# Attention operand stacks that outlive the projection block: constant rows and the first four units set up while the projection runs

## The reference

```python
x = x + attn0(layernorm(x))   # second norm with ln_g, ln_b inside; 16 heads of 16; causal softmax
x = x + mlp0(layernorm(x))    # 256 -> 2048 -> 256, 4-bit weights with scales, tanh-gelu
x = x + attn1(layernorm(x))   # 4 heads of 64, full softmax
x = x + moe1(layernorm(x))    # 64 experts of width 176, top 6, and a shared expert

# both attentions
Q, K, V = Xn @ Wq + bq, Xn @ Wk + bk, Xn @ Wv + bv
A = softmax(Q @ K.T * scale)              # per head
x = x + (A @ V) @ Wo + bo
```

## Time and profile before

| | us |
|---|---|
| median of 3 runs | 1477.82 |
| profiled execution, its own time | 1485.07 |
| its span, first to last instruction | 1483.2 |
| layer 0: projection block starts, attention block starts | 9.8, 88.7 |
| layer 1: projection block starts, attention block starts | 642, 706.0 |
| PE busy, share of the span | 86% |
| DVE, ACT, POOL | 54%, 29%, 34% |
| mean granted TensorE clock | 0.937 |

### The profile page before, as it was taken

The page is one execution under the profiler, slowest core; times in us unless marked ns, Lnnn a source line. Parts: engine busy times, 40 slices in busy tenths (PEclk is TensorE's granted clock), DMA queues, the critical chain, the costliest instruction groups (busy, mean ns, idle before and its releaser), DMA issues. The chain is left out here.

```text
span 1483.2 us, 22490 instructions
## 1 busy us (share of the span) xinstructions
PE 1268.3 (86%) x6348; PEld 888.1 (60%) x6348; DVE 806.5 (54%) x2185; ACT 431.8 (29%) x847; POOL 502.1 (34%) x602
## 2 busy tenths in 40 slices
PE   3859998987899999978799979748999999999950
PEld 2435555655688888845455565446777676676740
DVE  6747877743544343355445437984545444454437
ACT  1204544554533333222234422101222222222210
POOL 0042332333300000000400000867777777677720
PEclk9968989999999999989799989879999999999985
DMA  5598854800000000025543101019999999999949
GB/s 176 215 210 130 122 82 73 115 9 29 29 1 1 1 0 1 1 96 210 153 113 104 46 32 61 3 47 295 298 300 292 286 285 283 275 286 279 252 142 339
DMA packets 129927, 210.35 MB, mean 142 GB/s; under 512 B 26807, under 2 KB 59563, under 8 KB 129848
## 3 DMA queue, kind: packets, MB, share of 16 engines
q1 hardware_dynamic: 101911, 162.02, 40.8%
q0 software_dynamic: 15264, 34.78, 8.0%
q10 hardware_dynamic: 12672, 12.58, 2.4%
HBM read 168.92 MB, written 48.30 MB: 146 GB/s over the span
## 5 line engine op out<-in xcount | busy, mean ns | idle before, releaser
L1786 PE MATMUL experts_ps_gu<-experts_wgu,experts_xt 128*128 128x352 f32 x636 | 223.0, 473 | 13.7 <-DMA experts_wgu<-L_ffn_w_gate_up 6.3
L912 DVE TENSOR_REDUCE att_mx<-att_ps 128x1 f32<-128x512 f32 (+3 forms) x240 | 151.6, 652 | 87.1 <-PE att_ps L713 52.8
L713 PE MATMUL att_ps<-att_ks,att_qs 96*128 96x512 f32 (+4 forms) x384 | 157.2, 477 | 40.2 <-DMA att_ks<-k_parts 27.4
L1913 POOL DMA_INDIRECT y_parts<-experts_y,moe_target x159 | 161.5, 1015 | 69.2 <-DVE experts_picked L1877 34.9
L1907 POOL DMA_INDIRECT experts_x<-x_rows,moe_source x159 | 157.1, 988 | 62.8 <-issue 51.8
L1829 ACT ACTIVATE experts_xt<-experts_ps_x 128x256 f32<-128x256 f32 x159 | 60.9, 383 | 362.1 <-PE experts_ps_x L1775 362.1
L1807 PE MATMUL experts_ps_y<-experts_wd,experts_ht 96*128 96x256 f32 x636 | 163.4, 379 | 0.0
L1786 PEld LDWEIGHTS experts_ps_gu<-experts_wgu,experts_xt 128*128 128x128 f32 x636 | 111.7, 190 | 85.7 <-ACT experts_xt L1829 33.2
L849 ACT ACTIVATE att_pt<-att_ps 128x1024 f32<-128x1024 f32 (+3 forms) x160 | 121.7, 763 | 135.8 <-PE att_ps L735 135.4
L1860 DVE COPY experts_ht<-experts_ps_h 96x256 f32<-96x256 f32 x159 | 66.9, 421 | 149.5 <-PE experts_ps_h L1796 149.5
L713 PEld LDWEIGHTS att_ps<-att_ks,att_qs 96*128 96x128 f32 (+1 forms) x384 | 80.3, 214 | 92.7 <-issue 55.1
(11 more groups left out here) (217 smaller groups left out, 2265.6 us busy)
## 6 DMA issues: line engine op xcount, KB each, us to landing
experts_wgu<-L_ffn_w_gate_up SPq DMA_DIRECT2D x159, 352.0 KB, 8.7
experts_wd<-L_ffn_w_down SPq DMA_DIRECT2D x159, 176.0 KB
att_qs<-q_parts SPq DMA_DIRECT2D x112, 128.0 KB, 3.4
att_ks<-k_parts SPq DMA_DIRECT2D x112, 128.0 KB, 5.3
combine_got<-y_parts ACTq DMA_DIRECT2D x24, 512.0 KB, 8.8
q_parts<-qkv_hi SPq DMA_DIRECT2D x8, 512.0 KB, 2.9
q_parts<-qkv_lo SPq DMA_DIRECT2D x8, 512.0 KB, 3.7
k_parts<-qkv_hi SPq DMA_DIRECT2D x8, 512.0 KB, 3.4
```

Source lines behind the costliest of these rows:

```text
L713: ins = pe.matmul(out, qs[a][z][0:rows_a, h, i * P:(i + 1) * P], ks[a][z][0:rows_a, h, 0:width(i)], start=a == 0, stop=a == last_part and ...
L912: dve.tensor_reduce(mx[:, hs[0]:hs[-1] + 1, i], ps_1[:, (u.n * ng + g) % 2, 0:len(hs) * width(i)] .rearrange("p (h w) -> p h w", h=len(hs) ...
L1786: ins = pe.matmul(ps_gu[:, u.bank, 0:2 * FE], xt[:, u.bank, k, :], wgu[u.slot][:, k, :], start=k == 0, stop=k == KD - 1)
L1913: pool.indirect_dma_start(out=parts_dram[:, :], out_offset=bass.IndirectOffsetOnAxis(ap=target[:, n:n + 1], axis=0), in_=y[n % L][:, :], i ...
```

## The change

The stacks, `vs`, `w`, `bias` and their semaphores move into a class `Stacks`, allocated before the projection block and freed after the attention block. What was at the start of the attention block is now in the projection block:

```diff
 def project_qkv(..., heads, pitch, stacks, codes=None):
         @block.sync
             sp.dma_start(bv[:, :], w["bv"].partition_broadcast(P)).then_inc(v_weights_loaded, 16)
+            stacks.load_weights(sp)            # bias, w of the output projection
             if codes:
                 codes.load(sp)
...
-            chunks(sp, body)
+            for c in range(NCH):
+                body(c, True)
+                for n in FIRST_UNITS[c]:       # ((), (0, 1), (2, 3), ())
+                    stacks.load(sp, Unit(n))
+                    stacks.load_v(sp, Unit(n))
             sp.wait_ge(qk_stored, 16 * 4 * NCH)
             sp.wait_ge(v_stored, 16 * NCH)
         @block.gpsimd
             for i in range(CT):
                 pool.memset(v4[:, i, :, hd:hd + 1], 1.0).then_inc(v_columns_set, 1)
+            pool.wait_ge(v_columns_set, 1 + CT)
+            stacks.set_rows(pool)
+class Stacks:
+    def set_rows(self, pool):
+        for z in range(SLOTS):
+            for stacks in (self.qs, self.ks):
+                pool.memset(stacks[self.last_part][z][64:P, :, :].bitcast(F32), 0.0).then_inc(self.zero_rows_set, 1)
+        pool.wait_ge(self.zero_rows_set, 2 * SLOTS)
+        for z in range(SLOTS):
+            pool.memset(self.ks[self.last_part][z][NEG_ROW:NEG_ROW + 2, :, :].bitcast(F32), 1.0)\
+                .then_inc(self.rows_set, 1)
+        pool.wait_ge(self.rows_set, SLOTS)
 def attention(...):
         @block.sync
             def body(u):
                 v = u.plus(2)
-                if v.exists():
-                    if u.plus(-2).exists():
-                        sp.wait_ge(s2_done, (u.n - 1) * nx)
-                    load(v)
-                    if u.plus(-2).exists():
-                        sp.wait_ge(pv_done, (u.n - 1) * CT)
-                    load_v(v)
-                if u.n == 0:
-                    sp.dma_start(bias ...); sp.dma_start(w ...)
+                if v.exists() and v.n >= SLOTS:
+                    sp.wait_ge(s2_done, (u.n - 1) * nx)
+                    stacks.load(sp, v)
+                    sp.wait_ge(pv_done, (u.n - 1) * CT)
+                    stacks.load_v(sp, v)
                 load_maxima(u)
...
-            load(Unit(0))
-            load_v(Unit(0))
             loop(body)
         @block.gpsimd
-            set_rows(pool, qs, 0, 0)
-            for z in range(1, SLOTS):
-                set_rows(pool, qs, 0, z)
-                set_rows(pool, ks, 1, z)
         @block.tensor                          # scores_q no longer waits for stack_set
         @block.vector
-            set_rows(dve, ks, 1, 0)
             loop(body)
```

More of the change, by code:

```diff
@@ L467, in low, with __init__, load_weights, load @@
                           self.high_parts[n][:, :, :].bitcast(F32), ALU.subtract).then_inc(self.low_done, 1)
+FIRST_UNITS = ((), (0, 1), (2, 3), ())
+class Stacks:
+    def __init__(self, s, heads, pitch, parts, q_dram, k_dram, v_dram, wo, bo):
+        self.hu, self.hd = heads * UF // D, D // heads
+        self.rows = self.hu * pitch
+        self.parts, self.last_part = parts, len(parts) - 1
+        self.q_dram, self.k_dram, self.v_dram, self.wo, self.bo = q_dram, k_dram, v_dram, wo, bo
+        self.n_loads = sum(len(q) + len(k) for q, k in parts)
+        self.qs, self.ks = ([[s.sbuf(f"{n}s{a}_{z}", [P, self.hu, S], F32R) for z in range(SLOTS)]
+                             for a in range(len(parts))] for n in "qk")
+        self.vs = [s.sbuf(f"vs{z}", [P, CT, self.rows]) for z in range(SLOTS)]
+        self.w = s.sbuf("w", [P, KD, D])
+        self.bias = s.sbuf("bias", [P, D])
+        self.zero_rows_set = s.sem("zero_rows_set")
+        self.rows_set = s.sem("rows_set")
+        self.qk_loaded = [s.sem(f"qk_loaded{z}") for z in range(SLOTS)]
+        self.v_loaded = [s.sem(f"v_loaded{z}") for z in range(SLOTS)]
+        self.w_loaded = s.sem("w_loaded")
+    def set_rows(self, pool):
[7 more added lines that the diff above has]
+        pool.wait_ge(self.rows_set, SLOTS)
+    def load_weights(self, eng):
+        eng.dma_start(self.bias[:, :], self.bo.partition_broadcast(P)).then_inc(self.w_loaded, 16)
+        eng.dma_start(self.w[:, :, :], self.wo.rearrange("(k p) n -> p k n", p=P)).then_inc(self.w_loaded, 16)
+    def load(self, eng, u):
+        z, b, g = u.slot, u.batch, u.g
+        for a, pair in enumerate(self.parts):
+            for dram, stack, blocks in ((self.q_dram, self.qs, pair[0]), (self.k_dram, self.ks, pair[1])):
+                for row, half in blocks:
+                    src = dram[half][g * UF:(g + 1) * UF, b * S:(b + 1) * S]
+                    eng.dma_start(stack[a][z][row:row + self.hd, :, :].bitcast(F32),
+                                  src.rearrange("(h d) t -> d h t", d=self.hd)).then_inc(self.qk_loaded[z], 16)
+    def load_v(self, eng, u):
+        z, b, g = u.slot, u.batch, u.g
+        src = self.v_dram[b * S:(b + 1) * S, g * self.rows:(g + 1) * self.rows]
+        eng.dma_start(self.vs[z][:, :, :], src.rearrange("(j p) f -> p j f", p=P)).then_inc(self.v_loaded[z], 16)
@@ L482, in exists, with attention @@
         return 0 <= self.n < UNITS
[L485 to L493, removed]
+def attention(nc, tag, x_sb, ident, ident_bf, mask_q, stacks, pitch, causal, scale, normed,
+              codes=None, decoder=None, n_decoded=0):
+    hu, hd, rows = stacks.hu, stacks.hd, stacks.rows
+    parts, last_part, n_loads = stacks.parts, stacks.last_part, stacks.n_loads
+    qs, ks, vs, w, bias = stacks.qs, stacks.ks, stacks.vs, stacks.w, stacks.bias
+    qk_loaded, v_loaded = stacks.qk_loaded, stacks.v_loaded
     nt = CT * hu
     nx = nt // 2
-    rows = hu * pitch
-    last_part = len(parts) - 1
-    n_loads = sum(len(q) + len(k) for q, k in parts)
     with ExitStack() as ctx:
@@ L594, in _ @@
         def _(sp):
[L595 to L609, removed]
             def load_maxima(u):
@@ L698, in scores_q @@
                 z = u.slot
-                if step == 0 and part == 0 and not u.plus(-SLOTS).exists():
-                    for sem in stack_set[z]:
-                        pe.wait_ge(sem, 1)
                 if step == 0 and part == 0:
```

47 lines of the change are left out of this document (14 added, 33 removed).

## The result

The changed kernel takes 1499.42 us, the median of 4 runs (1493.48 to 1505.85), beside 1477.71 for the kernel before in the same session: a ratio of 1.0156, 95% interval [1.012, 1.0191]. It is slower, by some 22 us, and lies 0.8 us from the 1498.6 predicted. The terms of the sum did not come out that well: the memsets were put too small, the transfers of layer 0 and layer 1 too large, and the errors cancelled. That the total came so near is luck.

A forecast was written before the change was run, and what follows sets the result against it. PE bounds the kernel, busy 86% of the span, waiting for loads where attention begins. Terms 16.5 - 1.7 + 4.4 + 1.4 + 0.2 = 20.8 us on 1477.82 gave 1498.6, range 1487 to 1518.

The forecast's parts named there:

- Transfers of layer 0: Projection of layer 0: early unit loads delay later stores in one DMA line; first attention matmul at 115.4 against 98.92, +16.5.
- the second pair of units: Layer 0: loads of units 2 and 3, ahead of chunk 3's stores, take 17.6 us of the DMA line.
- The first pair: Layer 0: loads of units 0 and 1, behind chunk 1's stores, take 17.6 us of the DMA line.
- First maxima: Attention of layer 0: the first maxima no longer queue behind unit 3, so PE's 1.67 us wait goes, -1.7.
- Memsets: Early projection: POOL's memsets hold three 4-element DVE operations in layer 0, +1.4; shorter memsets in layer 1, +0.2.
- The halving for the doubt: Layer 0 memset term: half a memset for each of three held operations, halved again to give +1.4.
- Layer 1, +4.4: Attention of layer 1: transfers give -0.95 at the first matmul, but POOL's additions hold DVE, first maxima +4.4 instead.
- POOL's additions: Layer 1: sixteen additions start with the attention block and hold DVE's 4-element operation until the series ends at 722.6.
- If POOL lets DVE in after one addition, layer 1 gives -1: Alternative for layer 1's attention: DVE is not held to the end of POOL's additions, -1 instead of +4.4.
- The rival with memsets to the end of their series: Projections: memsets hold DVE until their series ends, 16.3 + 4.1 in place of 1.6, time 1517.4; chance 0.32.
- The loads slipping in: Both projections: loads run beside stores without delaying them, PE starts at 89.2 in layer 0, time 1466.8; chance 0.08.
- The base: Whole kernel: terms came from a profiled execution of 1485.07 us, 7.25 above the runs' median; forecast started from 1477.82.

The follow-up runs named there:

- late memsets: Changed kernel, but GpSimd's twelve memsets wait until VectorE has normalised the last chunk: 1486.94 us, 1.0053 to the kernel before.
- in the gaps: Changed kernel with memsets after the last normalisation, units 0 and 1 loaded behind stores of chunks 0 and 1, units 2 and 3 in attention: 1461.19 us, again 1459.23.
- the second profile: Changed kernel profiled once more, nothing altered: this execution took 1502.81 us; the rerun's median was 1500.14 us, ratio 1.0132 to the kernel before.
- with two: Changed kernel, memsets after the last normalisation, only unit 0 loaded early, issued by ScalarE on its own queue beside the last stores: 1466.01 us, ratio 0.9908.

## Why the prediction was right in its time, and where its steps were off

- **Transfers of layer 0, +16.5.** The mechanism is shown, step by step, by the windows of the kernel after and by the runs with late memsets and in the gaps. The size was 12.05 with late memsets, and 14.1 of the 22.1 in the changed kernel. The terms that were off are the second pair of units (14 us, or 16 in the changed kernel; 17.6 forecast) and the stores, at some 400 GB/s behind loads in place of 380 (7.5 to 8, 8.3 forecast). The first pair was 1 to 1.5 longer than forecast, and the stores of chunk 1 were done some 1 us earlier.
- **First maxima, -1.7.** From the first scores to the first L739 18.84 us, before 20.80: -2.0.
- **Memsets, +1.4 and +0.2.** The failed step. They cost 8.5 us up to the first transpose and 8.0 at the border; in layer 1 1.6 and 0.5. I named the 4-element operations alone, three of them by half a memset each, halved again. All held operations of that size together cost 2.6 us, near that count before halving; what was missing is L251, four tensor_scalars of 256 elements, 5.9 of the 8.5. The prediction listed the operations that looked like the one held in the earlier trace rows by size and not by form. The halving for the doubt had no row behind it either.
- **Layer 1, +4.4.** Also wrong. The transfers did nearly as forecast (block +6.5, +5.6 forecast; first matmul -0.5 in one profile of the changed kernel and 0.0 in the other and with late memsets, -0.95 forecast). The +5.4 for POOL's additions did not come: L925 was held 0.5 and 0.9 us, and the first L739 is 1.4 us earlier than before (0.8 in the second profile). The row of 2.50 us ending with POOL's series was read rightly; late operations end so too in all profiles that have one, as shown above. The error was to carry it over from an operation 8.6 us into the series to one 5 us into it: the first L925 of the kernel after ends 5.5 us ahead of its series' end. "If POOL lets DVE in after one addition, layer 1 gives -1" was the case that came.
- **The rival with memsets to the end of their series** (+13.1 before L140 ends) is refuted: L140 ended at 13.83, after one memset. **The loads slipping in** is refuted for one queue, and worth 3 us with two.
- **The total.** With the measured sizes, 22.1 at the first matmul, -2.0, and -1.4 in layer 1 make +18.7 (+19.2 from the second profile), beside +21.7 and +22.3 between the medians of the two sessions (intervals +17.7 to +28.2 and +14.9 to +23.9). The 20.8 forecast is so near since -4.4 on transfers, -0.3 on the first maxima, +6.6 on memsets, +2.05 for both together and -6.0 in layer 1 nearly cancel. The 0.8 us between forecast and result are no proof of the sum.
- **The base.** The profiled execution before lay 7.25 us over its median; it was used for the terms alone. Its expert part (485.64) and its attention of layer 0 (246.53) are the longest of all profiles; how much of the excess lies in either can't be told from one profile. Apart from the first maxima, no term comes from these two parts. One reading of the earlier trace rows was loose: the clock digit is 5 in the last slice too. Nothing rests on it.

## What to carry to other kernels

A transfer moved earlier is free only as far as the queue is empty at that time; what reaches into a later store pushes that store. Look for the windows with a DMA share near 0, put one unit in each, and leave the rest where its first use allows. Moving constants' memsets to an idle GpSimd is free here only while VectorE runs no tensor_scalar: list VectorE's operations beside them by form before size, and put the series behind the last of the held form. Loads moved forward can also stand ahead of a small transfer that a later step waits for, as units 2 and 3 did for the maxima. Test a hold seen in one row on other rows of the same kind before it becomes a term.

## What the runs showed of the hardware that I had not expected

- Stores that follow slow loads in the queue move at 395 to 410 GB/s, those that follow nothing at 375 to 385.
- SP took 4.4 to 6.2 us to issue the first four DMAs of a load behind a chunk's stores in the changed kernel and with late memsets, 1.75 with an empty queue; moved loads then also hold the issuing engine.
- A tensor_scalar of 4 elements 4.4 to 4.9 us into a series of 16 additions of POOL (0.69 us each) is held 0.3 to 0.5 us, less than one addition; one that starts 7.6 us into it or later to the end of the series (0.4 to 3.3 us). What makes the difference is open.
- The clock granted in the attention of layer 0 varies by itself, mean 0.90 to 0.93 between executions of one kernel, and shifts that stretch by 5 us; a gain of 3 us ahead of it can't be told from the end time.
